# Image filters behind an attention block: row filters issued ahead of column filters on three engines, and group statistics taken one image earlier

## The chip, the cores and the metric

One core of a Trainium2 chip runs the program. The metric is the device time of one launch in microseconds (us); of several runs the median is given. Of the engines, PE is TensorE (PEld its weight loads), DVE VectorE, ACT ScalarE, POOL GpSimd, SP SyncE, which here only issues transfers.

## The reference

x has the shape 8 x 512 x 128 x 128 in float32. Layer 0 normalises groups of 16 channels, runs a softmax attention over eight heads of 64 channels, and adds the result to x; call that x1. Layer 1, cut to what matters:

```
v  = groupnorm32(x1)                        # 16 channels x 128 x 128 per group
y  = up2(v, f_up) * 4 + bias                # rows, then columns: 128x128 -> 266x266
y  = clip(leaky(y, 0.2) * sqrt(2), +-256)
z  = down2(y, f_dn)                         # rows, then columns: 266x266 -> 128x128
out = x1 + z
```

## The kernel before

The 4096 images of 128 x 128 are handled in 32 **units** of 128 channels. A unit has two phases. The attention phase leaves x1 in SBUF (`xh`, one image row per partition). The filter phase then takes the unit's 128 images in 16 **batches** of 8 (`NBAT`, `IMG`); g numbers batches over the whole program, j is the batch in the unit and i the image in the batch. The change touches the filter phase alone. Each filter is a matrix multiplication with a banded matrix; float32 operands are split in two float16 halves, high and low, so that one product costs three matmuls (`mm3`).

For one image the work is:

- **rows up** (`up_rows`, PE, 3 matmuls of 266 columns from `xn_2` into `s1_ps`, a single PSUM bank), then `t1_high` (ACT, L547, rounds to float16), then `t1_low` (DVE, L860, the rest). Rows up run one batch ahead: while the columns of batch g are filtered, the rows of batch g+1 are. Since there is one bank, rows up of image i wait for `t1_low` of image i-1 (semaphore `s_t1`).
- **columns up** (`up_columns`, PE, 6 matmuls from `t1` into `y_ps`, two banks), then y (ACT, L573, scale and bias into `yb`), then the leaky step (DVE, L899), then the clip (POOL, L420). After each odd image POOL copies the ten columns beyond 256 away (`yc`, L423).
- **rows down** (`down_rows`, PE, 8 float32 matmuls of 64 or 69 columns, and 6 small ones `ps<-dr,xb` after each odd image), two images behind (`LAG`). Per pair of images: `down_high` (ACT, L559), `down_low` (DVE, L866).
- **columns down** (`down_columns`, 24 matmuls `ps<-dn,z` per half batch, at i = 2 and 4 for the batch before) and `add_out` (DVE, L875, at i = 3 and 5), which adds the result to x1.

Per batch there is a **remainder**: the rows beyond 256 of all eight images. POOL gathers them at the start of a batch (`t1r`, L449), in its queue behind the clip of the last image of the batch before; PE filters them at i = 0 (`ps<-up,t1r`), ACT takes them to `yr` (L579), DVE (L888) and POOL (L429 to L438) go on with them.

Each batch j+2 is also normalised: two ACT passes over eight images (`norm` L550, `xn_high` L554) and four POOL subtractions (`norm_low`, L444) into `xn_2`; rows up of the batch wait for the last of them. The scales come from the group's statistics, one chain per two batches, dealt out over the images: four `group_stats` (DVE, L794, 0.6 us each), `next_stats` (two small steps, L817 and L820), `group_average` (PE, a tiny matmul that stands in front of one rows up and waits for L820), `next_means`, `next_variance` (two steps), `sqrt1` (ACT, L541), `next_scales` (two steps, L840 and L842). For the unit's second group the whole chain lies in batch 0. DVE also reads statistics of the next unit's input (`c_stats`, L618) at i = 4 and 7.

The order of every engine's work is written out by hand: each engine has a function `batch(j, par, before, after)` with a loop over the eight images; `par` is j mod 2, and `before(n)` and `after(n)` say whether n batches precede or follow. A loop body holds two batches, so an even batch opens it. Every engine does its queue strictly in this order. In `batch` before, per image: PE columns up, rows up, rows down; ACT y, t1_high, then the pieces; DVE leaky, scales, t1_low, then the pieces.

Of the kernel before, what the change touches and what calls it, by code (L numbers as in the profile page):

```python
# [41 lines left out]
def attention_then_filters(nc, x, WaT, ba, WbT, bb_, WvT, bv, bias, fup, fdn, out):  # L42
# [8 lines left out]
    with ctx:  # L51
# [433 lines left out]
        def _(act):  # L485
# [7 lines left out]
            def unit(u):  # L493
# [51 lines left out]
                def t1_high(g, i, par, bank):  # L545
                    act.wait_ge(s_s1, IMG * g + i + 1)
                    act.activation(t1[:, par, 0, i, :], ps[:, bank, 0:UP], ACT.Copy).then_inc(s_th, 1)  # L547
# [18 lines left out]
                def batch(j, par, before, after):  # L566
                    g = NBAT * u + j
                    c0 = (u % CPB) * P + j * IMG
                    for i in range(IMG):
                        act.wait_ge(s_yp, IMG * g + i + 1)  # L570
# [4 lines left out]
                        if after(1):  # L575
                            t1_high(g + 1, i, 1 - par, 6)
# [10 lines left out]
                        if first and i == HALF:  # L587
                            sqrt1(slice(1, 2), 1)
# [27 lines left out]
        def _(dve):  # L616
# [93 lines left out]
            def unit(u, more):  # L710
# [179 lines left out]
                def batch(j, par, before, after):  # L890
                    g = NBAT * u + j
                    for i in range(IMG):
# [3 lines left out]
                        read_means = first and i == 3 or group and i == 6  # L896
# [5 lines left out]
                        if first and i == 5:  # L902
                            next_scales(q)
                        if i == 1 and par == 0 and before(1) and after(2):
                            next_scales(j // 2 + 1)
                        if after(1):
                            t1_low(g + 1, i, 1 - par, 6, (lambda: next_means(q)) if read_means else None)
# [5 lines left out]
                        if first and i < 2:  # L913
                            group_stats(1, 1, 2 * i)
                            last = group_stats(1, 1, 2 * i + 1)
                            if i == 1:
                                last.then_inc(s_st1, 1)
                                next_stats(q, 0)
                        if first and i == 2:
                            next_stats(q, 1)  # L920
                        if first and i in (3, 4):
                            next_variance(q, i - 3)
                        if par == 0 and after(4) and i in ((2, 4) if first else (0, 4)):
                            group_stats(j // 2 + 2, 1, i // 4)
                        if group and i in (0, 2):
                            last = group_stats(q, 1, 2 + i // 2)
                            if i == 2:
                                last.then_inc(s_st1, 1)
                        if group and i in (4, 5):
                            next_stats(q, i - 4)  # L930
                        if group and i in (6, 7):
                            next_variance(q, i - 6)
                        if before(1) and i in (3, 5):
                            add_out(g - 1, j - 1, i // 4, o_ps)
# [19 lines left out]
        def _(pe):  # L954
# [21 lines left out]
            def unit(u):  # L976
# [165 lines left out]
                def batch(j, par, before, after):  # L1142
                    g = NBAT * u + j
                    for i in range(IMG):
                        up_columns(g, i, par)
                        if after(1):
                            if i == 0:
                                pe.wait_ge(s_t1, IMG * (g + 1))
                            first = not before(1)
                            q = 1 if first else j // 2 + 2  # L1150
                            average = first and i == 3 or par and after(3) and i == 6
                            up_rows(g + 1, i, 1 - par, (lambda: group_average(q)) if average else None)
                        if i >= LAG:
                            down_rows(g, i - LAG, par)
                        elif before(1):
                            down_rows(g - 1, IMG + i - LAG, 1 - par)
# [64 lines left out]
```

## Time and profile before

| | |
|---|---|
| median of 3 runs | 16886.26 us (16883.11 to 16887.23) |
| profiled execution: its own time | 16875.47 us |
| profiled execution: span of the trace | 16873.7 us |
| mean granted clock of TensorE | 0.966 of full |
| busy: PE / DVE / ACT / POOL | 15189.3 / 12345.3 / 11219.7 / 8864.7 us |
| PE shares of the chain that ended last | 61%; DVE 14%, ACT 6%, POOL 3% |

Busy time is the union of an engine's instructions; span less busy time is idle, and an answer of the trace names what ended it. The 32 units follow each other every 522 to 528 us. Times inside the span are us from its start; all rows below lie in the unit whose first image's y starts at 8123.1.

### The profile page before, as it was taken

The page shows a single profiled execution, that of the slowest core. Times are in us where ns is not written, and L with a number is a line of the kernel's source. Part 1 is how long each engine was busy: PE and PEld are TensorE (multiplying, and loading weights), DVE is VectorE, ACT ScalarE, POOL GpSimd, SP SyncE. Part 2 cuts the span into 40 slices and gives each one's busy share as a digit, 9 for nine tenths or more (in the row PEclk, how much of TensorE's full clock was granted, in tenths as well). Part 3 has the DMA queues.
Part 4 walks back from the last instruction along what each step waited for, and adds up shares of the span by engine and source line. Part 5 has one row for each costly group of instructions (what it writes and reads, how often), then busy time and mean ns, then how long its engine had stood idle before and what let it go on. Part 6 is the DMA issues. An engine that isn't in the chain of part 4 may idle for free.

```text
span 16873.7 us, 461976 instructions
## 1 busy us (share of the span) xinstructions
PE 15189.3 (90%) x148708; PEld 12460.2 (74%) x148708; DVE 12345.3 (73%) x26154; ACT 11219.7 (66%) x19746; POOL 8864.7 (53%) x13589
## 2 busy tenths in 40 slices
PE   7898989989889898899988999899998999988898
PEld 5777777777777777777777777777777777777777
DVE  6777777777777777777777777777777777777776
ACT  5666666766666666666666666666666666666666
POOL 4554555545555455554555545555455554555545
PEclk9999999999999999999999999999999999999999
DMA  2122111121111211112111121111221112211120
GB/s 65 42 56 61 47 42 42 52 60 50 40 43 52 58 50 42 42 51 58 52 41 42 51 58 54 42 42 47 58 56 40 42 47 58 57 40 43 45 58 21
DMA packets 1147578, 821.47 MB, mean 49 GB/s; under 512 B 32068, under 2 KB 1080644, under 8 KB 1146308
## 3 DMA queue, kind: packets, MB, share of 16 engines
q1 hardware_dynamic: 1146308, 805.84, 17.2%
q8 instruction: 638, 10.45, 0.3%
q14 instruction: 632, 5.18, 0.1%
HBM read 537.30 MB, written 268.44 MB: 48 GB/s over the span
## 4 chain that ended last, share of the span: by engine, by line
PE 61%; DVE 14%; issue 12%; ACT 6%; POOL 3%; DMA 2%; DVEq 1%; ACTq 0%; POOLq 0%; SPq 0%
PE ps L956 59%; ACT yb L573 4%; DVE yb L899 3%; PE ps L1019 2%; DVE t L860 2%; DVE sth L794 2%; DVE z L866 2%; DVE stc L618 1%; ACT z L559 1%; DMA out<-xh 1%; POOL yb L420 1%; DVE yr L888 1%; DMA xh<-in_x 1%; ACT xn L554 0%; DVE nmr L842 0%
## 5 line engine op out<-in xcount | busy, mean ns | idle before, releaser
L420 POOL TENSOR_SCALAR yb<-yb 128x532 f32<-128x532 f32 x4096 | 2582.7, 631 | 4540.7 <-DVE yb L899 4540.2
L899 DVE SCALAR_TENSOR_TENSOR yb<-yb 128x532 f32<-128x532 f32 x4096 | 3255.0, 795 | 2123.6 <-ACT yb L573 2119.9
L573 ACT ACTIVATE yb<-ps,bias_b 128x532 f32<-128x532 f32 x4096 | 2875.7, 702 | 2374.6 <-PE ps L956 2336.4
L956 PE MATMUL ps<-dn_t,yb 128*128 128x64 f32 (+1 forms) x32768 | 4192.4, 272 | 0.0
L956 PEld LDWEIGHTS ps<-dn_t,yb 128*128 128x128 f32 x32768 | 4049.8, 194 | 84.0
L956 PE MATMUL ps<-up,t 128*128 128x266 f16 x24576 | 3490.8, 277 | 0.0
L956 PE MATMUL ps<-up,xn 128*128 128x266 f16 x12288 | 2133.8, 287 | 705.7 <-DVE t L860 449.7
L956 PEld LDWEIGHTS ps<-up,t 128*128 128x128 f16 x24576 | 2218.2, 100 | 301.9
L956 PEld LDWEIGHTS ps<-up,xn 128*128 128x128 f16 x12288 | 1059.1, 102 | 1417.2 <-DVE t L860 888.9
L403 POOL COPY xn<-xh 128x512 f32 x1024 | 1089.4, 1066 | 1767.1 <-PE ps L956 1073.4
L412 POOL TENSOR_TENSOR xh<-xh,pt 128x512 f32 (+1 forms) x1024 | 1693.0, 1653 | 523.0 <-DVE pt L777 520.0
L547 ACT ACTIVATE t<-ps 128x266 f16<-128x266 f32 x4096 | 1581.9, 387 | 543.4 <-PE ps L956 508.9
L860 DVE TENSOR_TENSOR t<-ps,t 128x266 f16<-128x266 f32 x4096 | 1731.7, 425 | 146.5 <-ACT t L547 75.2
L559 ACT ACTIVATE z<-ps 128x512 f16<-128x512 f32 x2048 | 1222.7, 597 | 802.6 <-PE ps L956 802.5
L866 DVE TENSOR_TENSOR z<-ps,z 128x512 f16<-128x512 f32 x2048 | 1402.9, 685 | 272.3 <-ACT z L559 233.3
L956 PEld LDWEIGHTS ps<-xn,pt 128*128 128x128 f32 x8192 | 1080.6, 194 | 551.1 <-issue 551.1
L956 PEld LDWEIGHTS ps<-gaug,p 128*128 128x128 f32 x8192 | 1070.1, 191 | 516.1 <-DVE pt L777 240.6
L444 POOL TENSOR_TENSOR xn<-xn 128x256 f16<-128x256 f32 x1792 | 1388.4, 796 | 3.8
L956 PE MATMUL ps<-yb,wbs 128*128 128x512 f32 x2048 | 1139.5, 647 | 99.8 <-ACT yb L495 95.8
L517 ACT ACTIVATE yb<-xc,sc 128x512 f32 (+1 forms) x1024 | 1198.5, 1170 | 0.0
L956 PE MATMUL ps<-xn,pt 128*128 128x128 f32 x8192 | 1101.1, 278 | 102.3 <-POOL xn L403 102.3
L495 ACT ACTIVATE yb<-xc 128x512 f32 (+1 forms) x1024 | 1098.0, 1082 | 77.0 <-issue 77.0
(147 smaller groups left out, 24501.5 us busy)
## 6 DMA issues: line engine op xcount, KB each, us to landing
xc<-in_x SPq DMA_DIRECT2D x512, 512.0 KB, 5.8
xh<-in_x SPq DMA_DIRECT2D x480, 512.0 KB, 6.4
out<-xh SPq DMA_DIRECT2D x480, 512.0 KB, 3.7
xh<-in_x SPq DMA_DIRECT2D x64, 256.0 KB, 2.9
out<-xh SPq DMA_DIRECT2D x64, 256.0 KB, 3.0
bias_b<-in_bias SPq DMA_DIRECT2D x1, 256.0 KB
bias_r<-in_bias SPq DMA_DIRECT2D x10, 2.0 KB
wa<-in_WaT SPq DMA_DIRECT2D x2, 16.0 KB
```

The source lines that it names most:

```text
L412: nc.gpsimd.tensor_tensor(xv, xv, zs_[par][:].rearrange("p w h m -> p w (h m)"), ALU.add).then_inc(s_x1, 1)
L420: nc.gpsimd.tensor_scalar(v, v, CLAMP, -CLAMP, ALU.min, ALU.max).then_inc(s_yc, 1)
L444: return nc.gpsimd.tensor_tensor(xn_2[:, par, 1, c, :], xn[:, c, :], xn_2[:, par, 0, c, :], ALU.subtract)
L495: act.activation(xcb[r].rearrange("p (w h) -> p w h", w=WB), xc_wh[:, bass.ts(k, WB), :], ACT.Copy).then_inc(s_xcb, 1)
L517: act.activation(xcb[r].rearrange("p (w h) -> p w h", w=WB), xc_wh[:, bass.ts(k, WB), :], ACT.Identity, bias=nm0).then_inc(s_xv, 1)
L547: act.activation(t1[:, par, 0, i, :], ps[:, bank, 0:UP], ACT.Copy).then_inc(s_th, 1)
L559: act.activation(z1[:, p // 2, 0, p % 2 * 2:p % 2 * 2 + 2, :, :].rearrange("p r c h -> p (r c h)"), dz_ps[p % 2], ACT.Copy).then_inc(s_zh, 1)
L573: act.activation(yb[:, i % YRING, :, :], y_ps[i % 2], ACT.Identity, scale=UPGAIN * GAIN, bias=bias_b[:, bass.ds(c0 + i, 1)]).then_inc(s_y, 1)
L860: nc.vector.tensor_tensor(t1[:, par, 1, i, :], ps[:, bank, 0:UP], t1[:, par, 0, i, :], ALU.subtract).then_inc(s_t1, 1)
L866: nc.vector.tensor_tensor(lo, dz_ps[p % 2], hi, ALU.subtract).then_inc(s_z1, 1)
L899: nc.vector.scalar_tensor_tensor(v, v, SLOPE, v, ALU.mult, ALU.max).then_inc(s_lr, 1)
L956: return nc.tensor.matmul(o, l, r, start=start, stop=stop, skip_group_check=share)
```

## The change

On PE, rows up of image i of the next batch are issued before columns up of image i, not after them. ACT does `t1_high` before y, and DVE does `next_scales` and `t1_low` before the leaky step. The steps of the group statistics move: in batch 0 all four `group_stats` are at i = 0, both `next_stats` at i = 1, the average at i = 2, both `next_variance` at i = 2, `sqrt1` at i = 3, `next_scales` at i = 4 (before: 0 and 1, 1 and 2, 3, 3 and 4, 4, 5); in odd batches the last `group_stats` is at i = 0, `next_stats` at 2 and 3, the average at i = 5 (before: 2, 4 and 5, 6). No instruction is added or taken away.

```diff
 ACT   for i in range(IMG):
+          if after(1):
+              t1_high(g + 1, i, 1 - par, 6)
           act.wait_ge(s_yp, IMG * g + i + 1)
...
-          if after(1):
-              t1_high(g + 1, i, 1 - par, 6)
...
-          if first and i == HALF:
+          if first and i == 3:
               sqrt1(slice(1, 2), 1)
 DVE
-          read_means = first and i == 3 or group and i == 6
+          read_means = first and i == 2 or group and i == 5
+          if first and i == 4:
+              next_scales(q)
+          if i == 1 and par == 0 and before(1) and after(2):
+              next_scales(j // 2 + 1)
+          if after(1):
+              t1_low(g + 1, i, 1 - par, 6, (lambda: next_means(q)) if read_means else None)
           v = yb[:, i % YRING, :, :]
           dve.wait_ge(s_y, IMG * g + i + 1 + YCREDIT)
...
+          if first and i == 0:
+              for p in range(4):
+                  last = group_stats(1, 1, p)
+              last.then_inc(s_st1, 1)
+          if first and i in (1, 2) or group and i in (2, 3):
+              for step in (range(2) if first else (i - 2,)):
+                  (next_variance if first and i == 2 else next_stats)(q, step)
           if group and i in (6, 7):
               next_variance(q, i - 6)
+          if par == 0 and after(4) and i in ((2, 4, 6) if first else (0, 4, 6)):
+              group_stats(j // 2 + 2, 1, i // 2 - 1 if first else (i + 1) // 3)
+          if group and i == 0:
+              group_stats(q, 1, 3).then_inc(s_st1, 1)
 PE    for i in range(IMG):
-          up_columns(g, i, par)
+          if i == 0:
+              pe.wait_ge(s_t1, IMG * (g + 1))
           if after(1):
-              if i == 0:
-                  pe.wait_ge(s_t1, IMG * (g + 1))
...
-              average = first and i == 3 or par and after(3) and i == 6
+              average = first and i == 2 or par and after(3) and i == 5
               up_rows(g + 1, i, 1 - par, ...)
+          up_columns(g, i, par)
           if i >= LAG:
               down_rows(g, i - LAG, par)
```

What PE has in its queue at the first image of a steady batch, before (`ps<-up,t` is columns up, `ps<-up,xn` rows up, `ps<-dn_t,yb` rows down, `ps<-up,t1r` the remainder):

```order
L956 MATMUL ps<-up,t 128x266 x6
L1148 ISA
L1074 REGISTER_ALU
L956 MATMUL ps<-up,xn 128x266 x3
L1096 ISA
L1099 ISA
L956 MATMUL ps<-dn_t,yb 128x64
L956 MATMUL ps<-dn_t,yb 128x69
L956 MATMUL ps<-dn_t,yb 128x64
L956 MATMUL ps<-dn_t,yb 128x69
L1159 ISA
L956 MATMUL ps<-up,t1r 80x266 x3
```

and now:

```order
L949 MATMUL ps<-up,xn 128x266 x3
L1076 ISA
L949 MATMUL ps<-up,t 128x266 x6
L1089 ISA
L1092 ISA
L949 MATMUL ps<-dn_t,yb 128x64
L949 MATMUL ps<-dn_t,yb 128x69
L949 MATMUL ps<-dn_t,yb 128x64
L949 MATMUL ps<-dn_t,yb 128x69
L1152 ISA
L949 MATMUL ps<-up,t1r 80x266 x3
```

Rows up went in front of columns up; the remainder stands where it stood.

DVE's queue from `down_low` of image 5 to the leaky step of image 6 in an even batch, before (L866 `down_low`, L875 `add_out`, L899 leaky, L860 `t1_low`):

```order
L866 TENSOR_TENSOR z<-ps,z 128x512
L873 REGISTER_ALU
L875 ISA
L875 TENSOR_TENSOR xh<-ps,xh 128x512
L898 REGISTER_ALU
L899 SCALAR_TENSOR_TENSOR yb<-yb 128x532
L857 REGISTER_ALU
L860 TENSOR_TENSOR t<-ps,t 128x266
```

and now:

```order
L866 TENSOR_TENSOR z<-ps,z 128x512
L873 REGISTER_ALU
L875 ISA
L875 TENSOR_TENSOR xh<-ps,xh 128x512
L857 REGISTER_ALU
L860 TENSOR_TENSOR t<-ps,t 128x266
L904 REGISTER_ALU
L905 SCALAR_TENSOR_TENSOR yb<-yb 128x532
```

`t1_low` passed the leaky step, and stands behind `down_low` and `add_out` as before.

DVE's queue in batch 0, from `t1_low` of image 0 to `next_means` of image 2, now:

```order
L860 TENSOR_TENSOR t<-ps,t 128x266
L905 SCALAR_TENSOR_TENSOR yb<-yb 128x532
L794 BN_STATS sth<-xh 128x6 x4
L857 REGISTER_ALU
L860 TENSOR_TENSOR t<-ps,t 128x266
L905 SCALAR_TENSOR_TENSOR yb<-yb 128x532
L888 SCALAR_TENSOR_TENSOR yr<-yr 80x266
L261 ISA
L817 BN_AGGR mvh<-sth 128x2
L261 ISA
L820 TENSOR_SCALAR mvh<-mvh 128x1
```

Before, two of the four statistics followed `t1_low` of image 0 and two that of image 1; now all four stand between `t1_low` of image 0 and that of image 1.

## Rows read from the trace of the kernel before

**Rows 1.** The page: its first line, and busy time by engine

```profile
span 16873.7 us, 461976 instructions
PE 15189.3 (90%) x148708; PEld 12460.2 (74%) x148708; DVE 12345.3 (73%) x26154; ACT 11219.7 (66%) x19746; POOL 8864.7 (53%) x13589
```

**Rows 2.** Waits over the span: us in total, times, longest us

```profile
PEld ps L956 <- DVE t L860: 888.9, 1587, 1.6
```

**Rows 3.** Timeline of PE, batches 6 (even) and 7 (odd); start us, us busy

```profile
8251.83 0.84 PE L956 MATMUL ps<-up,t 128*128 128x266 f16 x6
...
8254.44 0.51 PE L956 MATMUL ps<-up,t1r 128*80 128x266 f16 x3 [0.25 <-POOL t1r L449]
...
8258.87 0.52 PE L956 MATMUL ps<-up,xn 128*128 128x266 f16 x3 [0.78 <-DVE t L860]
...
8267.77 0.30 PE L956 MATMUL ps<-dr,xb 80*128 80x10 f16 x6
...
8269.21 0.52 PE L956 MATMUL ps<-up,xn 128*128 128x266 f16 x3 [0.44 <-DVE t L860]
...
8271.61 0.52 PE L956 MATMUL ps<-up,xn 128*128 128x266 f16 x3 [0.37 <-DVE t L860]
...
8272.96 0.84 PE L956 MATMUL ps<-up,t 128*128 128x266 f16 x6
...
8273.99 1.00 PE L956 MATMUL ps<-dn_t,yb 128*128 128x64 f32 x8
8274.83 0.51 PE L956 MATMUL ps<-up,t1r 128*80 128x266 f16 x3
...
8289.65 0.38 PE L956 MATMUL ps<-mvh,avg_p 128*128 128x2 f32 x2 [1.22 <-DVE mvh L820]
...
8293.09 0.84 PE L956 MATMUL ps<-up,t 128*128 128x266 f16 x6
```

**Rows 4.** Timeline of PE just before, at the other clock level

```profile
8247.52 1.82 PE L956 MATMUL ps<-dn_t,yb 128*128 128x64 f32 x8
8249.13 1.52 PE L956 MATMUL ps<-up,t 128*128 128x266 f16 x6
```

**Rows 5.** Timeline of all engines, last image of batch 5

```profile
8250.79 0.70 ACT L573 ACTIVATE yb<-ps,bias_b 128x532 f32<-128x532 f32 x1 [2.63 <-PE ps L956]
...
8251.52 0.71 DVE L899 SCALAR_TENSOR_TENSOR yb<-yb 128x532 f32<-128x532 f32 x1 [2.54 <-ACT yb L573]
...
8252.43 0.63 POOL L420 TENSOR_SCALAR yb<-yb 128x532 f32<-128x532 f32 x1 [3.35 <-DVE yb L899]
...
8253.83 0.47 POOL L449 COPY t1r<-t 128x160 f16<-128x160 f16 x1 [0.35 <-issue]
```

**Rows 6.** Timeline of all engines, images 5 and 6 of batch 6

```profile
8267.62 1.18 DVE L899 SCALAR_TENSOR_TENSOR yb<-yb 128x532 f32<-128x532 f32 x1
...
8268.10 0.60 ACT L559 ACTIVATE z<-ps 128x512 f16<-128x512 f32 x1 [0.23 <-PE ps L956]
...
8269.07 0.68 DVE L866 TENSOR_TENSOR z<-ps,z 128x512 f16<-128x512 f32 x1
...
8269.67 0.67 DVE L875 TENSOR_TENSOR xh<-ps,xh 128x512 f32 x1
...
8271.14 0.42 DVE L860 TENSOR_TENSOR t<-ps,t 128x266 f16<-128x266 f32 x1
```

**Rows 7.** Timeline of DVE, batch 0

```profile
8127.28 1.27 DVE L794 BATCH_NORM_STATS2 sth<-xh 128x6 f32<-128x512 f32 x2
...
8129.79 0.27 DVE L820 TENSOR_SCALAR mvh<-mvh 128x1 f32<-128x1 f32 x1
```

**Rows 8.** Timeline of all engines, end of batch 0

```profile
8143.99 1.76 POOL L444 TENSOR_TENSOR xn<-xn 128x256 f16<-128x256 f32 x2
...
8145.81 0.85 PE L956 MATMUL ps<-up,xn 128*128 128x266 f16 x3 [2.88 <-POOL xn L444]
```

**Rows 9.** Windows: length, busy time (count) of PE, PEld, DVE, ACT, POOL; granted clock; DMA

```profile
8145.80:8168.30 22.50, 21.27 (x224) 18.88 (x225) 14.21 (x29) 12.33 (x23) 10.02 (x19) 0.87 0.11 27
```

More of the change, by code:

```diff
@@ L901, in batch @@
                             remainder_leaky(g, par)
[L902 to L907, printed above, removed]
                         if i == 1 and before(1):
@@ L912, in batch @@
                             down_low(g, i // 2 - 1)
[L913 to L930, printed above, removed]
+                        if first and i == 0:
[5 more added lines that the diff above has]
+                                (next_variance if first and i == 2 else next_stats)(q, step)
                         if group and i in (6, 7):
                             next_variance(q, i - 6)
+                        if par == 0 and after(4) and i in ((2, 4, 6) if first else (0, 4, 6)):
+                            group_stats(j // 2 + 2, 1, i // 2 - 1 if first else (i + 1) // 3)
+                        if group and i == 0:
+                            group_stats(q, 1, 3).then_inc(s_st1, 1)
                         if before(1) and i in (3, 5):
```

## The prediction

> **What bounds the kernel now.** I read the page first: PE is busy for 90% of the span, and no other engine is above 73% [rows 1]. So time is lost where PE waits. The view of waits names the largest wait of a steady stage: weight loads of rows up stood for `t1_low` for 888.9 us [rows 2]. Then I read PE's timeline over an even and an odd batch of the filter phase and took each bracket as a wait. A group of matmuls stays busy for about 0.16 us after the next may start (columns up: 0.84 us busy, 0.68 us of the queue), so a wait is its bracket plus 0.16.
>
> The even batch lasts 8251.83 to 8272.96, 21.1 us. It waits 0.4 us for the remainder, 0.9 us at rows up 2, 0.6 at rows up 6, 0.5 at rows up 7 [rows 3], and some 0.5 in pieces too short for a bracket: 3.0 us. The odd batch lasts 20.1 us. Its large wait is that for the group average, 1.4 us [rows 3]; with 0.5 in short pieces 1.9. Without waits both would last about 18.1 us. The average also brings PE down to its lower clock in some batches: behind one such wait rows down took 1.82 us for 1.00 and columns up 1.52 for 0.84 [rows 3, 4], the 1.2 GHz level in place of 2.4.
>
> **What is moved, and what it gives.** No instruction is added, so every term is a wait. Let E be the moment at which columns up of image 7 leave PE.
>
> *The rows' own chain.* Matmul, `t1_high`, `t1_low`, next rows up: with rows up first, `t1_low` no longer stands behind the leaky step (0.71 us) of its image. That ends the waits at rows up 0, 1, 2 and 4. The average moves by one image and its two statistics steps by two, so that L820 is done at i = 3 and the average is asked for at i = 5: 1.4 us less per odd batch. This is what the change is built on, and I take it as true. Nothing on POOL or SP passes anything.
>
> *The remainder's chain.* From E: y, leaky, clip, the copy of the columns, `t1r`, remainder matmul. With E at 8250.46 (y starts 0.33 us after it), the rows give y 8250.79, leaky 8251.52, clip 8252.43, `t1r` 8253.83 and PE at 8254.44 [rows 3, 5]: 3.98 us. In the odd batch POOL does not reopen its loop (the 0.35 us "issue" in front of `t1r`), so it is about 3.65. None of these steps moves. But PE's cover for it does: before, rows up 7, rows down 5, columns up 0, rows up 0 and rows down 6, 0.34+0.99+0.68+0.34+0.84 = 3.2 us. Now rows up 7 lies ahead of E, and the cover is 2.85. Before, waits for `t1_low` lay in this stretch too and filled the rest. Now the wait at the remainder is 1.1 us in an even batch and 0.8 in an odd one (before 0.4 and 0).
>
> *`down_low` ahead of `t1_low`.* DVE still does `down_low` and `add_out` of image 5 before `t1_low` of image 6. From the end of rows down (PE free at 8267.92, 0.15 after its start) to `down_high` at 8268.10 is 0.18 us, then 0.60, `down_low` 0.69, `add_out` 0.68, `t1_low` 0.42, less 0.16 of overlap, plus 0.1 of signals [rows 3, 6]: 2.5 us. In it PE has rows up 6, columns up 6, rows down 4, 1.86 us. So rows up 7 wait 0.65 us, and a little more because the leaky step of image 5 meets `norm_low` on POOL (1.18 us for 0.71 [rows 6]) and `down_low` is behind it: 0.75. Before, the leaky step made the chain 0.63 longer, but columns up 7 were cover too; that is why the wait hardly shrinks. The same chain without `t1_low` makes columns down wait for `add_out` of image 3: 0.3 us, in odd batches 0.5, since `next_stats` now stands between.
>
> *Price of the contention.* The rows bound it: the leaky step gets between 0 and 0.47 us longer. I take half, in the 0.75 above. "SBUF — State Buffer" of the Trainium skill, section "SBUF: two separate sides", calls the pair of ports that DVE and GpSimd share an exclusive lock, with which the later one blocks entirely; by it the leaky step would lose the full 0.5 us in each batch with `norm_low`, and the sum would be some 0.25 us x 12 batches x 32 units = 96 us higher. The row above agrees in size, but shows a start in the midst of two POOL steps, so it does not fix the share.
>
> *Sum of a steady pair.* Even: 1.1 + 0.3 + 0.1 (rows up 6 behind two statistics) + 0.75 + 0.05 = 2.3 against 3.0: -0.7 us, to 20.4. Odd: 0.8 + 0.5 + 0.75 = 2.05 against 1.9: +0.15, to 20.3. Over a unit: six even batches -4.2, five odd ones +0.75. Batches 13 to 15 have no average and no `norm_low`, and so had little to lose: +0.4 in 13 and 14, and +0.3 in 15, where rows up are missing but the remainder waits. The low clock behind the average, worth 1.5 us where it comes, should go; I take half, -0.7.
>
> *The first two batches.* Here DVE sets the pace. Two statistics take 1.27 us [rows 7]. With four of them (2.5 us) between `t1_low` 0 and 1, I get leaky 0 done at 8125.9, the statistics at 8128.3, rows up 2 possible at 8128.7; but the average now stands in front of rows up 2 and L820 ends at about 8130.2 (before: 8130.06, in front of rows up 3 [rows 7]). So at 8130.5 PE is 2.5 us of its own work behind (one rows up, two columns up, one rows down). Carried through the batch, with `next_scales` at i = 4 behind `down_low` 0, the last `norm_low`, which ended at 8145.75 [rows 8], ends at about 8148.8. Rows up of batch 2 wait for it (8145.81 [rows 8]), and columns up 0 of batch 1, done in that wait before, now stand behind: 3.1 + 0.7 = +3.8 us. Both waits (now 4.7 and 4 us) are followed by a stretch at the lower clock; after the one of before the granted clock was 0.87 in the next 22.5 us [rows 9]. One more such stretch early in the batch costs between 0 and 3 us; I take 1.5. Together +5.3.
>
> Sum per unit: -4.2 + 0.75 + 0.4 + 0.3 - 0.7 + 5.3 = +1.85 us; x 32 = +59 us. On the profiled execution's own 16875.5 us this gives 16934; the median of the runs lies 10.8 us above it: **16945 us**, 0.35% slower. The attention phase is untouched.
>
> **Rivals.** (1) *Faster, by cover that I underrate.* If the wait at rows up 7 is not there (`down_high` or `add_out` comes sooner than in the row), each of 13 batches gains 0.75 us: -9.8 us a unit, -310 us, 16635. For it speaks only the size of the wait in [rows 2]; against it the order of the queue. Half of it gives 16790; a first batch that costs 2 us instead of 5.3 gives 16840. It decides from 1.9 us a unit, which is 0.15 us a batch, and my chains are no better than 0.1 each. (2) *The waits go and nothing follows*: all 888.9 us and the average's 1.4 us x 7 x 32 = 310 us come back: 15700. The remainder's chain, which rests on rows alone, speaks against it. (3) *No change*: steady gain and first-batch loss cancel within 0.2% (34 us), about what a measurement of this kernel can tell from none. My sum is 25 us from that. (4) *Slower by the clock*: every even batch now has a wait of 1.1 us at its start, and 0.75 near its end; if the clock falls there as behind the average, one stretch of 1.5 us in half of the batches is 12 us a unit, 17300. The lower level stood behind 1.4 us of wait [rows 4]; the even batch of before, with 0.9, shows none [rows 3]. [...]
>
> **How the numbers follow.** My sum, slower by over 0.2%: 0.47; with the clock rival 0.03: **0.50**. Within 0.2%: **0.21**. Faster: 0.27 for a milder first batch or shorter chains, 0.02 for the second rival: **0.29**. Range: ±0.1 us on each of five waits in 13 batches adds to about ±2.5 us a unit, the first batch another ±2, the lock +3: from 16800 to 17080.
>
> **What would show it.** Right: at the remainder brackets of about 0.9 (even) and 0.6 (odd); rows up 2 and 4 without a bracket; the average without one; rows up 7 with about 0.6 <- DVE t; in batch 0 rows up 2 waiting for L820 for over 1.5 us, and rows up of batch 2 about 3 us later after the unit's first y. Even batches 20.4 us, odd ones 20.3. Wrong: if `t1r` shows no larger wait, or if the first two batches together grow by less than 2 us, the kernel is faster.

## The result and the profile after

| | before | after |
|---|---|---|
| median (5 runs of each) | 16886.26 us | 16976.78 us (16947.98 to 17000.26) |
| profiled execution: its own time | 16875.47 us | 16970.38 us |
| mean granted clock of TensorE | 0.966 | 0.962 |

The change makes the kernel slower by 0.53%: ratio 1.0053, 95% interval 1.0039 to 1.0068. The time lies within the predicted range and on the side that was given the largest chance; the centre of the forecast (16945) was 32 us too low.

The page of the kernel after, its first line and busy times, against [rows 1]:

```profile
span 16968.7 us, 462040 instructions
PE 15123.1 (89%) x148708; PEld 12717.0 (75%) x148708; DVE 12416.2 (73%) x26154; ACT 11331.0 (67%) x19746; POOL 8942.5 (53%) x13589
```

PE does the same 148708 matmuls in 66 us less of busy time, and the span is 95 us longer: PE stands still for 161 us more. The view of waits says for whom (us in total, times, longest us):

```profile
PEld ps L949 <- DVE t L860: 368.9, 544, 0.9
...
PE ps L949 <- DVE t L860: 324.5, 544, 1.0
PE ps L949 <- POOL t1r L449: 320.8, 448, 1.4
...
PE ps L949 <- DVE mvh L820: 147.0, 32, 4.6
PE ps L949 <- POOL xn L444: 111.6, 32, 3.5
```

The wait that led before, weight loads of rows up for `t1_low`, fell from 888.9 to 368.9 us [rows 2]. In its place stands the remainder: matmuls waited 320.8 us for `t1r`, which before were 39.8 us in 128 waits. The group average (L820) is asked for without a wait in all batches but the first, where PE now waits 4.6 us for it.

The timeline of PE in the kernel after, an even batch (6) and an odd one (7), the same places as [rows 3]:

```profile
8303.10 0.51 PE L949 MATMUL ps<-up,t1r 128*80 128x266 f16 x3 [0.93 <-POOL t1r L449]
...
8318.51 0.52 PE L949 MATMUL ps<-up,xn 128*128 128x266 f16 x3 [0.62 <-DVE t L860]
...
8323.16 0.51 PE L949 MATMUL ps<-up,t1r 128*80 128x266 f16 x3 [0.59 <-POOL t1r L449]
...
8333.26 0.92 PE L949 MATMUL ps<-dn,z 128*128 128x64 f16 x24 [0.31 <-DVE xh L875]
...
8334.10 0.36 PE L949 MATMUL ps<-mvh,avg_p 128*128 128x2 f32 x2
...
8338.84 0.52 PE L949 MATMUL ps<-up,xn 128*128 128x266 f16 x3 [0.47 <-DVE t L860]
...
8343.82 0.39 PE L949 MATMUL ps<-up,t1r 128*80 128x266 f16 x2 [0.92 <-POOL t1r L449]
```

Rows up 2, 4 and 6 have no bracket (2 and 6 had one [rows 3]), and the average has none. What remains in each batch is a wait at the remainder (0.93, 0.59) and one at rows up 7 (0.62, 0.47), and in the odd batch one of columns down for `add_out` (0.31).

The timeline of the kernel after in batch 0, which answers to [rows 7, 8]:

```profile
8172.03 2.46 DVE L794 BATCH_NORM_STATS2 sth<-xh 128x6 f32<-128x512 f32 x4
8174.42 0.42 DVE L860 TENSOR_TENSOR t<-ps,t 128x266 f16<-128x266 f32 x1
...
8176.13 0.27 DVE L820 TENSOR_SCALAR mvh<-mvh 128x1 f32<-128x1 f32 x1 [0.16 <-DVE mvh L817]
...
8176.45 0.59 PE L949 MATMUL ps<-mvh,avg_p 128*128 128x2 f32 x2 [4.59 <-DVE mvh L820]
...
8176.90 0.83 PE L949 MATMUL ps<-up,xn 128*128 128x266 f16 x3
8177.52 1.53 PE L949 MATMUL ps<-up,t 128*128 128x266 f16 x6
...
8195.00 1.30 POOL L444 TENSOR_TENSOR xn<-xn 128x256 f16<-128x256 f32 x2
...
8196.36 0.85 PE L949 MATMUL ps<-up,xn 128*128 128x266 f16 x3 [3.49 <-POOL xn L444]
```

Four statistics in a row (2.46 us) hold up `t1_low` of image 1 and then L820, and PE stands 4.59 us in front of rows up 2. Rows up take 0.83 and columns up 1.53 us behind it, the 1.2 GHz level (0.51 and 0.84 in the rows above). The same holds behind the 3.49 us wait for the last `norm_low`. The windows of the kernel after (columns as in [rows 9]; batch 0 from its first y, then the next 24 us):

```profile
8170.70:8196.30 25.60, 16.36 (x132) 13.89 (x131) 17.23 (x35) 12.26 (x22) 10.63 (x21) 0.86 0.01 2
8196.30:8220.40 24.10, 23.19 (x239) 20.54 (x240) 15.36 (x32) 14.03 (x26) 10.67 (x21) 0.87 0.11 28
```

The granted clock is the third number from the end. Before, the first of these stretches had 0.98 over 22.70 us.

**Where the time went.** From the trace I took the start of the first y of every batch, in all 32 units, and averaged the lengths from batch to batch (us). The last two columns belong to the experiments e6 and e8, told below.

| batches | before | after | e6 | e8 |
|---|---|---|---|---|
| 0 and 1 together | 45.27 | 49.24 | 45.07 | 49.32 |
| 4, 6, 8, 10 (even), each | 21.15 | 20.42 | 20.68 | 19.90 |
| 7, 9 (odd), each | 20.13 | 20.33 | 19.67 | 19.83 |
| 13 and 14 together | 38.74 | 39.65 | 38.74 | 38.96 |

Measured from the end of `t1_low` of image 7 of batch 0 to the first y of batch 2, the start of a unit took 45.39 us before and 50.85 after, +5.5. Of this, 1.5 us lie ahead of the unit's first y, which came 0.12 us behind that `t1_low` and now comes 1.61 behind it: PE's wait for it stands ahead of rows up 0 and, with the new order, ahead of columns up 0 too. Even batches 2 to 12 give back 4.4, odd batches 3 to 11 cost 0.2, 13 and 14 cost 0.9. The profiled span is 95 us, 3.0 us a unit, longer; the 0.8 us that are left lie in batch 15.

### The profile page after: what moved, and what is told of

Same layout as the page of the kernel before. It is cut to its first block, busy times and chain, and to the rows that moved or that the text cites. A ratio compares the mean times of both kernels' runs of the same rounds, so it can differ in the third digit from the quotient of the medians.

```text
span 16968.7 us, 462040 instructions
## 1 busy us (share of the span) xinstructions
PE 15123.1 (89%) x148708; PEld 12717.0 (75%) x148708; DVE 12416.2 (73%) x26154; ACT 11331.0 (67%) x19746; POOL 8942.5 (53%) x13589
## 4 chain that ended last, share of the span: by engine, by line
PE 57%; DVE 14%; issue 10%; ACT 8%; POOL 6%; DMA 2%; DVEq 1%; POOLq 1%; ACTq 0%; SPq 0%
PE ps L949 55%; ACT yb L575 4%; DVE yb L905 4%; DVE xh L875 3%; ACT z L559 2%; PE ps L1012 2%; POOL yb L420 2%; DVE t L860 1%; DVE sth L794 1%; DMA out<-xh 1%; POOL t1r L449 1%; POOL xb L436 1%; DVE stc L618 1%; ACT xn L554 1%; DMA xh<-in_x 1%
## 5 line engine op out<-in xcount | busy, mean ns | idle before, releaser
L905 DVE SCALAR_TENSOR_TENSOR yb<-yb 128x532 f32<-128x532 f32 x4096 | 3171.5, 774 | 1384.9 <-ACT yb L575 1384.8
L949 PE MATMUL ps<-up,t 128*128 128x266 f16 x24576 | 3532.5, 280 | 0.0
L949 PEld LDWEIGHTS ps<-up,t 128*128 128x128 f16 x24576 | 2405.0, 98 | 445.3
L949 PE MATMUL ps<-up,xn 128*128 128x266 f16 x12288 | 2145.3, 288 | 578.2 <-DVE t L860 324.5
L860 DVE TENSOR_TENSOR t<-ps,t 128x266 f16<-128x266 f32 x4096 | 1739.2, 427 | 771.2 <-ACT t L547 645.8
L949 PEld LDWEIGHTS ps<-up,xn 128*128 128x128 f16 x12288 | 1032.4, 104 | 811.5 <-DVE t L860 368.9
L866 DVE TENSOR_TENSOR z<-ps,z 128x512 f16<-128x512 f32 x2048 | 1407.0, 687 | 207.6 <-ACT z L559 166.7
```

What stands on the lines that cost most here:

```text
L860: nc.vector.tensor_tensor(t1[:, par, 1, i, :], ps[:, bank, 0:UP], t1[:, par, 0, i, :], ALU.subtract).then_inc(s_t1, 1)
L866: nc.vector.tensor_tensor(lo, dz_ps[p % 2], hi, ALU.subtract).then_inc(s_z1, 1)
L905: nc.vector.scalar_tensor_tensor(v, v, SLOPE, v, ALU.mult, ALU.max).then_inc(s_lr, 1)
L949: return nc.tensor.matmul(o, l, r, start=start, stop=stop, skip_group_check=share)
```

## The experiments

Every kernel computes the same as before and after. "Old order" means columns up, rows up on PE, with y ahead of `t1_high` on ACT and the leaky step ahead of `t1_low` on DVE. Each ratio is to the kernel before, run on the same chip. The experiments ran on four chips, on which the kernel before took 16872 to 16882 us (16886 beside the kernel after), so a difference in us between two of these kernels is only good to about 15 us. Edits are shown against the kernel after unless the text says otherwise. My theory: the new order shortens PE's cover for the chain to `t1r` and leaves `down_low` ahead of `t1_low`, which uses up what the earlier average gives, and batch 0 makes the loss. The first rival: the new order gives time of its own, and only the statistics in batch 0 take it back. The second rival: the lower clock makes the difference.

### The two halves of the change: e1 and e2

e1 is the kernel before with the new order alone; the statistics stay at their old images (against the kernel after, so these lines undo its moves):

```diff
-                        read_means = first and i == 2 or group and i == 5
-                        if first and i == 4:
+                        read_means = first and i == 3 or group and i == 6
+                        if first and i == 5:
                             next_scales(q)
...
-                            average = first and i == 2 or par and after(3) and i == 5
+                            average = first and i == 3 or par and after(3) and i == 6
```

> The changed order of rows and columns on PE, ACT and DVE, with every statistics step where it stood before. My theory (the order trades the row wait for waits at the remainder and behind down_low; the statistics in batch 0 and the average are separate terms): even batches 20.4 us as in the changed kernel; odd ones about 21.0, since the average at image 6 waits about 1.5 us for a step that stands behind down_low of image 5, which takes the place of the wait at rows up 7; the first two batches about 2.5 us shorter than in the changed kernel, because only two statistics stand in front of t1_low of image 1. Sum: 17060, slower than the changed kernel (16977) by 0.3 to 0.8%. Rival (the moved statistics alone make the kernel slower, the new order is a gain): below 16886.

Measured: 17276.85 us, ratio 1.0244 (1.0227 to 1.0261). The direction held, the size did not. Even batches took 20.3 to 20.4 us, as in the kernel after, odd ones 22.5 to 22.7. The timeline of PE in e1, an odd batch:

```profile
8473.13 0.38 PE L956 MATMUL ps<-mvh,avg_p 128*128 128x2 f32 x2 [1.86 <-DVE mvh L820]
...
8473.72 0.84 PE L956 MATMUL ps<-up,t 128*128 128x266 f16 x6
8474.40 1.47 PE L956 MATMUL ps<-dn_t,yb 128*128 128x64 f32 x8
...
8476.32 1.54 PE L956 MATMUL ps<-up,t 128*128 128x266 f16 x6
```

Ahead of columns up, rows up ask for the average 0.68 us earlier, so its bracket grew from 1.22 [rows 3] to 1.86 us, and behind it the clock fell: columns up took 1.54 us. The odd batches 3 to 11 show the lower level in 85 of 160 cases, 9.9 us a unit in all, which can cost up to 5 us. The forecast had 21.0 us for an odd batch, without a term for the clock, and took the first two batches as 2.5 us shorter than in the kernel after; they were 0.5 shorter (48.77 for 49.24). With the average at i = 6 the new order is the worst kernel of the study; the earlier average is not a gain added to it but what makes it bearable.

e2 is the other half: all statistics moved, old order.

```diff
-                        if i == 0:
-                            pe.wait_ge(s_t1, IMG * (g + 1))
+                        up_columns(g, i, par)
                         if after(1):
+                            if i == 0:
+                                pe.wait_ge(s_t1, IMG * (g + 1))
...
                             up_rows(g + 1, i, 1 - par, ...)
-                        up_columns(g, i, par)
```

(and the same on ACT and DVE.)

> The moved statistics with the old order of rows and columns. My theory: odd batches lose the average's wait of 1.4 us but get the waits at rows up 6 or 7 that even ones have, so 19.9 us for 20.1; even ones stay at 21.1; the first two batches get 1.5 to 2 us longer. Sum: 16886 plus or minus 60. Rival (the statistics' place is the loss): above 16977. Second rival (the average's 1.4 us comes back whole): 16886 - 6 x 1.4 x 32 + 60 = 16680.

Measured: 16771.12 us, ratio 0.994 (0.9924 to 0.9957): faster where I expected no change. Not only odd batches gained (20.13 to 19.66 us), even ones did as much (21.15 to 20.68), and the trace of e2 suggests why. The timeline of PE in e2, end of an odd batch and start of an even one:

```profile
8289.37 0.52 PE L949 MATMUL ps<-up,xn 128*128 128x266 f16 x3 [0.30 <-DVE t L860]
...
8292.86 0.51 PE L949 MATMUL ps<-up,t1r 128*80 128x266 f16 x3
```

Part of the average's wait has become one at rows up 7. In the old order these come behind columns up 7, so the wait falls into the cover of the remainder's chain, and the remainder has no bracket (before: 0.25 [rows 3]). The same 0.5 us of wait (0.30 and the 0.16 that a bracket leaves out) serves two chains. The new order, added to this, costs 16977 - 16771 = 206 us, so as a whole it gives no time of its own, and the first rival falls.

### The statistics in steady batches and in batch 0: e6 and e7

e6 is the old order with the moved statistics in odd batches only; batch 0 is as before. e7 is the kernel after with batch 0's statistics at their old images. Both differ from the kernel after by this edit, and e6 by the old order besides:

```diff
-                        if first and i == 0:
-                            for p in range(4):
-                                last = group_stats(1, 1, p)
-                            last.then_inc(s_st1, 1)
...
+                        if first and i < 2:
+                            group_stats(1, 1, 2 * i)
+                            last = group_stats(1, 1, 2 * i + 1)
...
-                            average = first and i == 2 or par and after(3) and i == 5
+                            average = first and i == 3 or par and after(3) and i == 5
```

> The kernel before, with the statistics moved in the odd and even steady batches alone; batch 0 keeps its old steps and the order of rows and columns is the old one. The run with all statistics moved gave 16771; in its trace the last norm_low of batch 0 ends 23.7 us after the unit's first y, against 22.7 before, and a stretch at the lower clock stands early in the batch that was not there. If those are the price of the four statistics in front, this kernel gives 1.0 us and most of 2.7 us of low clock a unit back: 16660 (16640 to 16720), the best so far. Rival (batch 0 costs nothing net): 16771 within 25.

Measured: 16674.8 us, ratio 0.9882 (0.9865 to 0.9898). As expected (16660): this is what the change contains of gain, 1.2%.

> The changed kernel with batch 0's statistics at their old images; order and odd batches as changed. The last norm_low of batch 0 ended 27.2 us after the unit's last t1_low of the row phase in the changed kernel, 25.1 with the new order alone and 22.7 before. So batch 0's statistics cost 2.2 us a unit under the new order: 16977 - 70 = 16905 (16870 to 16930), still not faster than before. Then the order by itself costs 2.3 us a unit in batch 0. Rival (the steps of batch 0 are neutral, the order is all): 16977 within 25.

Measured: 16825.94 us, ratio 0.9973 (0.9963 to 0.9983): 151 us less than the kernel after, where I expected 70. Batches 0 and 1 together took 45.85 us for 49.24, 3.4 us a unit; batches 2 to 14 are the same to 0.02. The other 1.2 us a unit lie between the last y of a unit and the first of the next (198.7 us for 199.9), where nothing was edited; I did not find out why. It is a general limit of these comparisons: from the last y of a unit to the end of `t1_low` of image 7 of the next batch 0, a stretch that no edit touches, the kernels of this study take 197.1 us (e7) to 199.2 (e5), and 2 us a unit are 67 us in all. Part of the 3.4 is the clock: from 18 us ahead of the first y to the first y of batch 2, the granted clock was at its lower level for 25.9 us a unit in the kernel after, 21.4 in e7 and 17.8 before. A us at that level costs at most half a us (columns up: 1.53 us for 0.84), so up to 2.2 of the 3.4.

e6 and e7 differ in the order alone: 151 us for the new order. The batches show it where nothing else happens: even 20.68 to 20.42, odd 19.67 to 20.33. In the start of a unit, measured as above, the order costs 2.3 us (45.20 for 47.46), and in batches 13 to 15 another 1.7.

### The two steady waits: e3, e4 and e5

e3 is the kernel after with the second `add_out` (L875) at i = 7, so that it no longer stands in front of the `t1_low` for which rows up 7 wait:

```diff
-                        if before(1) and i in (3, 5):
+                        if before(1) and i in (3, 7):
```

> The changed kernel with the second add_out of a batch at image 7 instead of 5. My theory: the wait at rows up 7 comes from down_low and add_out of image 5 in front of t1_low of image 6; without add_out the chain is 1.9 us against 1.86 us of matmuls, so that wait falls from 0.7 to about 0.1 us in each of 13 batches, nothing takes its place, and the time is 16730 to 16820. Rival (rows up 7 wait because the leaky step of image 5 meets POOL's norm_low, with down_low behind it): the wait stays, 16977 within 30.

Measured: 16821.55 us, ratio 0.997 (0.9958 to 0.9981), 155 us less than the kernel after, at the edge of what I expected. Rows up 7 have no bracket any more. The remainder has more of one, 424.8 us in 448 waits for 320.8: a wait that PE does not spend at rows up 7 no longer fills the time until `t1r` is there. And once a unit, behind its last y, columns down now wait 2.0 us for the `add_out` that was put at i = 7. Even batches took 19.98 and odd ones 20.05 us.

e4 is the kernel after with the remainder's rows one image later on PE, and `yr` on ACT with them:

```diff
+                        if i == 1:
+                            pe.wait_ge(s_o, 2 * (g - 1 if before(1) else g) + OCREDIT)
+                            remainder_rows(g, par)
...
-                        if i == 0:
-
-                            pe.wait_ge(s_o, 2 * (g - 1 if before(1) else g) + OCREDIT)
-                            remainder_rows(g, par)
```

> The changed kernel with the remainder's rows on PE between columns up and rows down of image 1, and the remainder's activation on ACT behind y of image 1. My theory: the chain from columns up 7 to the remainder (4.0 us even, 3.65 odd) now has 3.9 us of matmuls as cover, so the waits of 1.1 and 0.8 us at the remainder go; t1_low of image 0, behind down_low and the input statistics of image 7, gives back 0.3. Sum: 0.6 us a batch x 15 x 32 = 290 us less than the changed kernel, 16690 (16600 to 16800), faster than before too. Rival (the odd 1 us of each batch is bound by something else behind the remainder, such as yr and the small remainder steps on POOL that rows down 3 wait for): the wait moves to those steps and the time stays within 60 us of 16977.

Measured: 16876.51 us, ratio 1.0003 (0.9994 to 1.0013), 100 us less than the kernel after, not 290. The wait for `t1r` (320.8 us) is gone altogether, and about two thirds of it came back elsewhere: PE's waits for `t1_low` rose from 324.5 us in 544 to 531.8 in 979. Even batches took 20.20 and odd ones 20.27.

e5 has both edits.

> Both edits on the changed kernel: second add_out at image 7 and the remainder's rows at image 1. Each alone gave about 155 and 100 us. If the remainder's chain was the cover that took back part of the first edit (the wait in front of the remainder grew from 1.3 to 1.5 us when rows up 7 no longer waited), the two together give more than their sum: 16977 - 155 - 100 - 60 = 16660 (16600 to 16720). Rival (they draw on the same slack): 16820, no better than the first alone.

Measured: 16957.15 us, ratio 1.0051 (1.0034 to 1.0068). A clear miss: each edit gains alone, and together they gain 20 us, which their intervals can't tell from nothing. The timeline of PE in e5, an even and an odd batch:

```profile
8304.85 0.52 PE L949 MATMUL ps<-up,xn 128*128 128x266 f16 x3 [1.15 <-DVE t L860]
...
8325.14 0.52 PE L949 MATMUL ps<-up,xn 128*128 128x266 f16 x3 [1.24 <-DVE t L860]
```

One large wait is left in each batch, at rows up 1: 1.15 us for 0.93 + 0.62 in the even batch, 1.24 for 0.59 + 0.47 in the odd one. It is for `t1_low` of image 0, which on DVE stands behind `down_low`, `add_out` and the statistics step of image 7. The work put at i = 7 did little harm while PE stood at the remainder in front of rows up 1; it does when the remainder is out of the way. That reading is argued from the order of DVE's queue; no run tested it apart.

### Cover put back: e8 to e12

If cover is what the new order lost, columns up 7 back in front of rows up 7 should give it back, ahead of both waits. e8 is the kernel after with the old order for image 7 alone, on all three engines; on PE:

```diff
+                        if i == 7:
+                            up_columns(g, i, par)
...
                             up_rows(g + 1, i, 1 - par, ...)
-                        up_columns(g, i, par)
+                        if i < 7:
+                            up_columns(g, i, par)
```

> The changed kernel, but at image 7 columns up, y and leaky go ahead of rows up, t1_high and t1_low on all three engines, so that rows up 7 lie behind the moment from which the remainder's chain runs. If the lost cover is what the order costs in steady batches, each of 15 batches gets 0.3 us shorter (not the whole 1.0 us by which columns up 7 can start earlier, since DVE reaches the leaky step of image 7 only after a statistics step): 16977 - 140 = 16835 (16740 to 16920). Rival (the cover does not matter): 16977 within 30.

Measured: 16718.31 us, ratio 0.9906 (0.9889 to 0.9922), 259 us less than the kernel after, where I expected 140. One image of eight carries more than the whole cost of the new order. The clock is not what it gives back: the low-clock time at the start of a unit is 24.6 us for 25.9. e9 adds batch 0's statistics at their old images (the edit of e7).

> Columns first at image 7 only, and batch 0's statistics at their old images. The two edits act in different batches, so their gains (259 and 151 us against the changed kernel) should add: 16977 - 410 = 16570 (16540 to 16610). Rival (the wait behind norm_low at the end of batch 0 absorbs one of them): above 16650.

Measured: 16639.16 us, ratio 0.9855 (0.9839 to 0.9872). I had expected the gains of e7 and e8 to add. They do not in full: 338 of 151 + 259 = 410 us. Of the 72 us that are missing, 37 lie in the stretch between units that no edit touches, and about 24 in the filter phase: with columns first at image 7, the old statistics shorten the start of a unit by 2.7 us (50.93 to 48.19) in place of 3.4 (50.85 to 47.46). The timeline of e9, end of an even batch and start of the next, shows what became of the two waits:

```profile
8167.47 1.80 POOL L420 TENSOR_SCALAR yb<-yb 128x532 f32<-128x532 f32 x2
...
8168.67 0.51 PE L958 MATMUL ps<-up,xn 128*128 128x266 f16 x3 [1.01 <-DVE t L862]
...
8169.44 0.26 POOL L423 COPY yc<-yb 128x40 f32<-128x40 f32 x1 [0.17 <-POOL yb L420]
...
8169.71 0.47 POOL L449 COPY t1r<-t 128x160 f16<-128x160 f16 x1
...
8170.54 0.51 PE L958 MATMUL ps<-up,t1r 128*80 128x266 f16 x3
```

The `t1r` copy ends at 8170.18 and the remainder's matmul starts at 8170.54 in turn. The one wait left is 1.01 us at rows up 0 of the next batch, which follow rows up 7 with only rows down between them: the image where the order changes back has no columns up to cover its own `t1_low`.

So e10 tried to cover that too: e9 with columns first at image 0 as well. e11 is e10 with the remainder at image 1.

```diff
-                        if i == 7:
+                        if i in (0, 7):
                             up_columns(g, i, par)
...
-                        if i < 7:
+                        if 0 < i < 7:
                             up_columns(g, i, par)
```

> As the run before, with columns first at image 0 too; rows first stay at images 1 to 6. With columns first at 7 alone, rows up 0 of the next batch wait 0.9 to 1.2 us for t1_low of image 7 with columns up 0 (0.68 us) behind them. If columns up 0 go into that wait, the stretch from columns up 7 to the remainder is bound by the remainder's chain alone (4.0 us even, 3.65 odd) in place of 4.3 to 4.4: 0.3 to 0.6 us a batch, 16570 - 150 = 16420 (16350 to 16520). Rival (t1_low of image 0, now behind the leaky step again, makes rows up 1 wait for as much): 16570 within 40.

Measured: 16775.76 us, ratio 0.9935 (0.9918 to 0.9951), 137 us more than e9: a miss in sign. The wait at rows up 0 fell to 0.31 us, but the leaky step of image 0 now comes earlier and meets the `t1r` copy. The timeline of e10, start of an odd batch:

```profile
8236.60 0.69 DVE L907 SCALAR_TENSOR_TENSOR yb<-yb 128x532 f32<-128x532 f32 x1
8236.65 0.96 POOL L449 COPY t1r<-t 128x160 f16<-128x160 f16 x1
...
8237.76 0.51 PE L958 MATMUL ps<-up,t1r 128*80 128x266 f16 x3 [0.80 <-POOL t1r L449]
```

Medians over batches 4 to 11 of all units tell what this collision costs, and what it does not explain. In e9 and e10 alike the copy starts 3.3 us behind y of image 7. It takes 0.47 us in e9, and 0.82 (even) and 0.96 (odd) in e10; the remainder's matmul follows y of image 7 by 3.92 and 4.18 us in e9, by 4.28 and 4.44 in e10. That is 0.36 and 0.26 us later, and over 14 batches in 32 units it comes to the 137 us. The collision costs 0.35 and 0.49 us a batch. Without it the matmul would come at about 3.93 and 3.95, no earlier than in e9 in an even batch and 0.2 us earlier in an odd one: most of the gain of 0.3 to 0.6 us a batch was not there to be had, because I had taken the chain from before, where the copy starts 3.04 and 2.77 us behind y.

> The run before with the remainder's rows at image 1. The remainder's chain then has 0.34 + 0.68 us more of cover. But in the run with the remainder and the second add_out both moved, rows up 1 waited 1.3 us for t1_low of image 0, which stands behind down_low, the statistics and the leaky step of image 7 on DVE. By that, DVE's queue is the next bound and nothing is gained: 0 to 60 us above or below the run before. Rival (the remainder's chain still decides): 100 us faster.

Measured: 16805.92 us, ratio 0.9952 (0.9936 to 0.9969), 30 us more than e10, as expected: the remainder's wait is not the thing to move.

e12 is e9 with batch 0 in the old order throughout; on PE (against the kernel after):

```diff
+                        rows_first = before(1) and i < 7
+                        if not rows_first:
+                            up_columns(g, i, par)
...
-                        up_columns(g, i, par)
+                        if rows_first:
+                            up_columns(g, i, par)
```

> Rows first only in batches 1 to 14 and only at images 0 to 6; batch 0 entirely as before, image 7 columns first. From the last t1_low of the row phase to the first y of batch 2 the traces show 45.2 us with batch 0 as before under the old order, and 48.2 us in the run with rows first in batch 0 and its old statistics (0.3 of it because y 0 now follows rows up 0). If the order by itself costs 2.6 us in batch 0, this gives 16639 - 85 = 16555 (16530 to 16600), the best of all. Rival (batch 0 ends where it ends because of norm_low, whatever the order): 16639 within 25.

Measured: 16568.92 us, ratio 0.9818 (0.9805 to 0.9832), the fastest of all, 408 us below the kernel after and close to the 16555 expected. The start of a unit takes 45.85 us for the 48.19 of e9. Its low-clock time at the start of a unit is back to 17.5 us, and its mean granted clock is 0.969. Against e6 (16674.8), which has the same statistics and the old order everywhere, e12 gains 106 us: at images 0 to 6 of batches 1 to 14 the new order is a gain, and only at image 7 and in batch 0 is it a loss.

## Why the prediction held, and which terms were off

**Bound and steady batches: right.** Predicted 20.4 (even) and 20.3 us (odd), measured 20.42 and 20.33. The chain from E (columns up 7 leaving PE) to `t1r` came out link by link. The timeline of the kernel after, batch 6 into 7:

```profile
8319.85 0.70 ACT L575 ACTIVATE yb<-ps,bias_b 128x532 f32<-128x532 f32 x1 [0.39 <-PE ps L949]
...
8320.58 0.71 DVE L905 SCALAR_TENSOR_TENSOR yb<-yb 128x532 f32<-128x532 f32 x1 [0.33 <-ACT yb L575]
...
8321.49 0.63 POOL L420 TENSOR_SCALAR yb<-yb 128x532 f32<-128x532 f32 x1 [1.03 <-DVE yb L905]
...
8322.56 0.46 POOL L449 COPY t1r<-t 128x160 f16<-128x160 f16 x1
```

From y to the remainder's matmul it is 3.31 us, and 0.3 from E to y, against the 3.65 of the forecast; in even batches the same stretch has a median of 3.65 us before and after, 3.98 with the 0.33 from E to y, as forecast. Brackets 0.93 and 0.59 for the 0.9 and 0.6 predicted. e8 shows that the missing cover is the cause: put back, both waits go, and what comes in their place, a wait of about 1 us at rows up 0, costs less: even and odd batches fall to 19.90 and 19.83 us, and batches 13 and 14 return to 38.96 us against 38.74 before.

**Rows up 7: right.** Predicted a bracket of about 0.6 in both kinds of batch, measured 0.62 and 0.47; e3 took away one of the instructions in that chain, and the wait with it. The half share of the port contention in this term is right only as an average: the leaky step of image 5 took a median of 1.13 us in even batches and 0.72 in odd ones (1.19 in both before), so even batches lose nearly the full price and odd ones next to nothing.

**The average: right for the kernel after, incomplete as an argument.** It has no bracket, the odd batches came out as summed, and the low clock behind it is gone: before, batch 5 took 0.7 us more than batches 7 and 9 and had the lower level in 14 of 32 units, and now it takes no more than they do (taken: 0.7 us a unit). But I weighed the move of the average inside the new order alone. In the old order it is worth 0.5 us in odd and even batches alike (e2, e6), so my small net gain hid a gain of 212 us (before to e6) and a loss of 151 (e6 to e7, part of it at the start of a unit). The step from e7 to the kernel after is another 151, the statistics of batch 0. These three are steps on one way from before to after and so must add up; on the way over e2 the same statistics of batch 0 cost 96 us (e6 to e2) and the order 206. The size of each part depends on what is there already.

**Batch 0: total right, split wrong.** Predicted +5.3 us, measured +5.5; PE waited 4.75 and 3.65 us (brackets 4.59 and 3.49, plus 0.16) where 4.7 and 4 were forecast. The forecast has the later first y in it, as its leaky step of image 0 ends at 8125.9. I put 3.8 on the chain and 1.5 on the clock, and let the last `norm_low` end 3.1 us later; measured from that `t1_low`, it ended 4.1 us later on average (26.9 for 22.8). Some of the loss that I had put behind it came ahead of it. The low-clock time there grew by 8.1 us a unit (17.8 to 25.9), which is up to 4 us; e7 takes 4.5 of the 8.1 away, e12 all of it. Up to three quarters of the term may be the clock; the runs don't separate it further, so that this total came out right is in part luck.

**Batches 13 to 15: the mis-sized term.** The sum had +0.4 for 13 and 14 together and +0.3 for 15; 13 and 14 measured +0.9, and what follows the first y of batch 15 +0.8. I took the new waits of these batches as half covered, and e8, which is only 0.2 above before in 13 and 14, shows that nearly all of their cost is the missing cover of image 7. This 1.0 us a unit is 32 us, nearly all of the distance of the forecast from the result; the other terms were off by 0.2 us a unit or less each (even batches -4.4 for -4.2, odd ones with their clock +0.2 for +0.05, the start +5.5 for +5.3).

**The rivals.** Cover that I underrate: no, the chains held to 0.1 us. No new waits: no. The clock rival, where half of the batches would pay for the lower level behind a wait of 1.1 us: not borne out. The kernel after shows no stretch at the lower level between the second batch and the end of the filter phase, in any unit, though each batch has two waits of 0.6 to 1.1 us. e1 does show them behind its bracket of 1.86 us, in 85 of 160 cases. "TensorE: Matmul & The Clock Gate" of the Trainium skill, section "HAM oscillation — how this bites in real kernels", tells of a kernel that is back at the lower clock behind every one of its repeated waits; the waits there are longer than those of a steady batch here. The traces of the kernel after show the like behind the 4.75 and 3.65 us waits at the start of a unit, in every unit, and not behind waits of 1.1 us or less.

**The range.** Its lower end is the plain sum of its terms, -4.5 us a unit. Its upper end is not: 2.5 + 2 + 3 us would give 17185; 17080 is about what the root of their squares gives.

**What stays open:** the 1.2 us a unit outside the filter phase between the kernel after and e7, and more generally why the stretch between units differs by up to 2 us from kernel to kernel, and how batch 0's loss divides between chain and clock.

## What to carry to other kernels

Before swapping two groups in an in-order queue, name the instruction from which each late chain starts and add up the queue's work between it and the consumer: whatever moves in front of the start is cover lost, and the wait comes back elsewhere. Swap only where a chain gains from it (here images 0 to 6 of batches 1 to 14, e12), not where the swap sits at the head of another chain. Two fixes that each gain may share one cover, as in e5, so measure them together before keeping both.

## What the runs showed of the hardware

The time of a POOL copy, which I took as fixed, is not. In e10 the `t1r` copy took a median of 0.83 us for 0.47 in e9, by the view of the tile (duration in ns min/median/max). Of e10:

```profile
L449 POOL COPY t1r<-t x512: 451/830/1032, 255.7 to 16747.4; 128x160 f16<-128x160 f16 x171
```

Of e9:

```profile
L449 POOL COPY t1r<-t x512: 455/466/478, 255.3 to 16608.3; 128x160 f16<-128x160 f16 x171
```

Where DVE's leaky step had started 0.05 us earlier, it kept its 0.69 us and the copy took 0.96. The timeline of the kernel after, start of an even batch, shows the reverse:

```profile
8302.49 0.47 POOL L449 COPY t1r<-t 128x160 f16<-128x160 f16 x1 [0.35 <-issue]
8302.55 0.97 DVE L905 SCALAR_TENSOR_TENSOR yb<-yb 128x532 f32<-128x532 f32 x1
```

The copy came first by 0.06 us and kept its 0.47, and the leaky step took 0.97 for 0.71. The later of the two loses, 0.3 to 0.5 us. By "SBUF — State Buffer" of the Trainium skill, section "SBUF: two separate sides", whichever of the two starts first holds the shared ports for its whole instruction and the other is blocked. These rows agree in who loses. In size they stay 0.15 us below a full block: the copy took 0.96 us where 0.64 of blocking and its own 0.47 would be 1.11, the leaky step 0.97 where 0.41 and 0.71 would be 1.12. I had priced that lock only on the leaky step; in e10 it fell on the short copy in front of PE.
